# 137 products of constants added to TensorE's queue, in a transformer block with eight experts

## The chip, the cores and the metric

One core of a Trainium2 chip. The metric is the time of one launch on the device, in microseconds (us). TensorE is called PE, VectorE DVE, ScalarE ACT, GpSimd POOL and SyncE SP, as the profile does.

## The reference, cut to what matters

```
def reference(x, tok_weight, q_proj, k_proj, v_proj, o_proj, wg, W1, b1, W2, b2):
    h = take(tok_weight, x)                       # x 32x128 ids, h 32x128x256 f32
    h = h + attention(layernorm(h), ...)          # 16 heads of 16, causal softmax
    h = h + experts(layernorm(h), ...)
    return h
# experts: logits = xf @ wg (8 experts), top-1, a token's rank within its expert,
#   capacity int(4096 / 8 * 1.25) + 1 = 641; tokens past it give 0
#   y = gelu(xe @ W1 + b1) @ W2 + b2             # 256 -> 1024 -> 256
#   out = y[slot] * softmax weight of the token's expert
```

All of it is float32.

## The kernel before, in words

The kernel runs in two blocks: `attention_phase`, then `expert_phase`. Between them all engines join.

**Attention** takes the 32 sequences in 16 groups of two (`NG` = 16, 256 tokens each). The program is written as 22 steps of 8 slots (`step(n, i)`, `for s in range(UNITS)`), and every engine goes through the same steps in its own queue, with semaphores between them. A group passes through the steps as through a pipeline. On PE, for group g: the four transposes of its normalised rows `xn` (`turn4`, slot 7 of step g-1, L522), its projections Q in slot 1, K in slot 2 and V in slot 7 of step g (`project`, `passes`, L559: twelve matmuls of 256 columns each, as three products of a high and a low part), its scores from slot 4 of step g+1 on (L587 adds the mask `maskb` through an identity, L590 multiplies), the shifted scores (L604) and the products with V (L701) some slots later. Then come, in steps g+3 and g+4, the transposes of the values (`turn_values`, L574), their normalised form `on` (L522), the output projection (L559), and in steps g+4 and g+5 the transposes of the second norm `xn2` (L522), the router's logits (L665, eight matmuls of 8 columns) and in step g+6 the ranks (L673 to L677). In the last steps (19 to 21) only these last parts of groups 15 and 14 are left.

Around PE: ScalarE copies each result out of its bank (`xth`, `qp`, `kp`, `va`, `oth`, `x2t`) and takes the exponential. VectorE makes the low parts (`xtl`, `otl`), the rests (`qr`, `kr`), the statistics, the rows' maxima `mx` of each score bank (L781), and the routing up to `oh` and `pos`. GpSimd makes the third parts of q and k, gathers the embedding rows and stores the routed rows to `slots` by indirect DMA (L366). SP writes the parts of q and k to DRAM and reads them back stacked (`qs`, `ks`, L301); the scores need them. It also writes blank rows to `slots` in steps 0 to 5.

At the start, ahead of step 0: PE transposes the token ids (L528), waits for the four attention weights (`d_w`), transposes them (L534, sixteen transposes) and the biases (L538), then the rows of group 0.

**Experts**: eight in turn. For each, `xs` rows are loaded, normalised (`xne`, L1153) and transposed on PE (`turn`, L1071, three turns of four transposes), split into high and low parts (`xh`, `xl`), multiplied with W1 (L1110, sixteen units of six matmuls of 324 columns) and, after the gelu, with W2 (L1127, four of 24), transposed back (L1083), and stored by indirect DMA (L993). The turns of an expert run within the expert before it; those of expert 0 stand alone, ahead of its first matmul. ScalarE and VectorE split the weights (L1008, L1145).

`trib` is a 128x128 bf16 triangle of ones and `maskb` a 128x4x128 bf16 mask. Both are made by GpSimd at the start (`g_set` counts). `bPV` and `bS[0]` are banks of PSUM: the product with V first writes `bPV` in step 3; the scores last write `bS[0]` in step 17.

Of the kernel before, what the change touches and what calls it, by code (L numbers as in the profile page):

```python
# [21 lines left out]
P = 128  # L22
F32 = mybir.dt.float32
F32R = mybir.dt.float32r
BF16 = mybir.dt.bfloat16
# [49 lines left out]
def lm_block(nc, x, table, wq, wk, wv, wo, wg, W1, b1, W2, b2, out):  # L75
    NB, S = x.shape
    D = table.shape[1]
    E, _, F = W1.shape
    H, DK = 16, D // 16
    N = NB * S  # L80
    CAP = int(N / E * 1.25) + 1
    KC = D // P
    GB = 2
    NG = NB // GB
    GT = GB * S
    QUADS = H // 4
    PARTS = 3
    KS_ROWS = 6 * DK
    SCALE = float(DK) ** -0.5
    NT = 6  # L90
    TS = -(-CAP // NT)
    TS += TS % 2
    SL = NT * TS
    NH = SL // 2
    FC = F // P
    NOWHERE = 1 << 20
    assert S == P and TS <= P and NH <= 512

    slots = nc.dram_tensor("rows_of_slots", [E * SL, ROW], F32)
    qparts = [nc.dram_tensor(f"q_parts{i}", [PARTS, D, GT], BF16) for i in range(RING)]  # L100
    kparts = [nc.dram_tensor(f"k_parts{i}", [PARTS, D, GT], BF16) for i in range(RING)]
    outf = out.rearrange("b s d -> (b s) d")

    with ExitStack() as whole:
        def sb_in(scope):
            return lambda name, shape, dt: scope.enter_context(nc.sbuf_tensor(name, shape, dt))

        sb = sb_in(whole)

        def sem(name):  # L110
            return whole.enter_context(nc.semaphore(name))

        bank = {n: whole.enter_context(nc.psum_tensor(n, [P, 512], F32))
                for n in ("S0", "S1", "C0", "C1", "PV", "M0", "M1", "M2")}
        bS = [bank["S0"], bank["S1"]]
        bC = [bank["C0"], bank["C1"]]
        bPV, bM0, bM1, bM2 = bank["PV"], bank["M0"], bank["M1"], bank["M2"]

        identf = sb("identf", [P, P], F32)
        raw = [sb(f"w_raw{q}", [P, 2 * KC * F], F32) for q in range(2)]  # L120

        biases = sb("biases", [P, E * (FC + KC)], F32)
        halfneg = sb("halfneg", [P, 8], F32)
        d_raw = [sem(f"d_raw{q}") for q in range(2)]

        def load_w1(eng, e, q):

            eng.dma_start(raw[q][:, 0:KC * F].rearrange("p (k f) -> p k f", k=KC),
                          W1[bass.ds(e, 1)].rearrange("a (k p) f -> p (a k) f", p=P)).then_inc(d_raw[q], 16)

        def load_w2(eng, e, q):

            eng.dma_start(raw[q][:, KC * F:].rearrange("p (c d) -> p c d", c=FC),
                          W2[bass.ds(e, 1)].rearrange("a (c p) d -> p (a c) d", p=P)).then_inc(d_raw[q], 16)

        load_half = (load_w1, load_w2)

        attention_phase(nc, sb_in, sem, locals())
        expert_phase(nc, sb_in, sem, locals())


def attention_phase(nc, sb_in, sem, v):
# [15 lines left out]
    with ExitStack() as scope:  # L158
        sb = sb_in(scope)

        identb = sb("identb", [P, P], BF16)
        maskb = sb("maskb", [P, 4, S], BF16)
        trib = sb("trib", [P, P], BF16)
        onesb = sb("onesb", [P, P], BF16)
        eps_of = sb("eps_of", [P, GB * E], I32)
        iota8 = sb("iota8", [P, GB, E], F32)
# [349 lines left out]
        def _(pe):  # L516
# [6 lines left out]
                return last  # L523


            pe.wait_ge(g_set, 1)
            pe.wait_ge(v_xf, 1)
            pe.transpose(bM0[:, 0:NB], xf[:, :], identf[0:NB, 0:NB]).then_inc(pe_id, 1)  # L528
            pe.wait_ge(d_w, 64)
            for m in range(4):  # L530
                dst = [bM1, bM2, bS[0], bS[1]][m]
# [9 lines left out]
            pe.wait_ge(v_idt, 1)  # L541
            pe.wait_ge(v_xn, 1)
            turn4(bM0, xn).then_inc(pe_T, 1)

            pe.wait_ge(a_wh, 4)
            pe.wait_ge(v_wl, 4)
# [30 lines left out]
            def step(n, i):  # L577
                for s in range(UNITS):

                    g, u = shift_unit(n, i, s, S_LAG)  # L580
                    if g:
                        if u == 0:
# [50 lines left out]
                    g = group(n, i + 1)  # L633
                    if g and s == 7:
                        wait(pe, v_xn, g.times(1, 1))
                        wait(pe, v_qr, g.times(1))
                        wait(pe, v_on, g.back(4).times(GB, 1))
                        turn4(bM0, xn).then_inc(pe_T, 1)
# [64 lines left out]
                        last.then_inc(pe_PV, 1)  # L703

            steps(pe, step)

        @block.vector
        def _(dve):
# [202 lines left out]
def expert_phase(nc, sb_in, sem, v):  # L911
    D, E, KC, F, FC, SL, NT, TS, NH, N = (v[n] for n in ("D", "E", "KC", "F", "FC", "SL", "NT", "TS", "NH", "N"))
    slots, outf = v["slots"], v["outf"]
    bS, bC, bPV, bM0, bM1, bM2 = (v[n] for n in ("bS", "bC", "bPV", "bM0", "bM1", "bM2"))
    identf, biases, raw, d_raw, load_half = (v[n] for n in ("identf", "biases", "raw", "d_raw", "load_half"))
    up_bank = [bS[0], bS[1], bC[0], bC[1]]
    down_bank = [bPV, bM2]
    turn_bank = [bM0, bM1]
# [8 lines left out]
    with ExitStack() as scope:  # L927
# [133 lines left out]
        @block.tensor  # L1061
        def _(pe):
            def turn(e, r):

                wait(pe, v_exn, e.times(NT, 2 * r + 2))

                wait(pe, v_xl, e.times(TURNS, r // 2))
                for k in range(KC):
                    for j in range(2):
                        at = (k * 2 + j) * TS  # L1070
                        last = pe.transpose(turn_bank[r % 2][:, at:at + TS], xn[:, 2 * r + j, k * P:(k + 1) * P],  # L1071
                                            identf[0:TS, 0:TS])
                last.then_inc(e_turn, 1)

            def back(e, j):


                wait(pe, a_yt, e.times(DOWN, KC * (1 + j // (NT // 2))))
                wait(pe, v_ys, e.times(NT, j - 1))
                if j < 2:  # L1080
                    wait(pe, a_gelu, e.times(NU, NU))
                for c in range(KC):
                    last = pe.transpose(back_bank[j % 2][0:TS, c * P:(c + 1) * P], yt[:, c, j * TS:(j + 1) * TS],  # L1083
                                        identf[:, :])
                last.then_inc(e_back, 1)


            for r in range(TURNS - 1):
                turn(expert(0, 0), r)

            def step(n, i):
                e, e0, e1 = expert(n, i), expert(n, i - 1), expert(n, i + 1)
                q = e.slot
                w1 = [w[q][:, 0:KC * F].rearrange("p (k f) -> p k f", k=KC) for w in (wh, wl)]
                w2 = [w[q][:, KC * F:].rearrange("p (c d) -> p c d", c=FC) for w in (wh, wl)]
                xt = [xh[q], xl[q]]
                ht = [hh, hl]
                three = ((0, 0), (0, 1), (1, 0))
                for u in range(NU):
                    half, f = divmod(u, FC)  # L1100

                    wait(pe, v_xl, e.times(TURNS, TURNS - 1 + half))
                    wait(pe, v_wel, e.times(PIECES, PIECES // 2))
                    wait(pe, a_gelu, e.times(NU, u - 3))
                    if u in (2, 3):

                        wait(pe, v_ys, e.times(NT, u - 3))
                    terms = [(k, a, b) for k in range(KC) for a, b in three]
                    for m, (k, a, b) in enumerate(terms):
                        last = pe.matmul(up_bank[u % 4][:, 0:NH], w1[a][:, k, f * P:(f + 1) * P],  # L1110
                                         xt[b][:, k, half * NH:(half + 1) * NH],
                                         start=(m == 0), stop=(m == len(terms) - 1))
                    last.then_inc(e_up, 1)
                    if isinstance(n, int) and i == 0 and u == 0:
                        turn(e, TURNS - 1)
                    if e0:
                        for j in ((3, 4), (5,))[u] if u < 2 else ():
                            back(e0, j)
                for v in range(DOWN):
                    half, d = divmod(v, KC)  # L1120

                    wait(pe, v_hl, e.times(NU, FC * (half + 1)))
                    wait(pe, v_wel, e.times(PIECES, PIECES))
                    wait(pe, a_yt, e.times(DOWN, v - 1))
                    terms = [(c, a, b) for c in range(FC) for a, b in three]
                    for m, (c, a, b) in enumerate(terms):
                        last = pe.matmul(down_bank[v % 2][:, 0:NH], w2[a][:, c, d * P:(d + 1) * P],  # L1127
                                         ht[b][:, c, half * NH:(half + 1) * NH],
                                         start=(m == 0), stop=(m == len(terms) - 1))
                    last.then_inc(e_down, 1)  # L1130
                    for j in ((), (), (0, 1), (2,))[v]:
                        back(e, j)
                    if e1 and v < TURNS:
                        turn(e1, v)

            steps(pe, step)
            for j in (3, 4, 5):
                back(expert(0, E - 1), j)
# [99 lines left out]
```

## Time and profile before

| what | us |
|---|---|
| median of 3 runs | 629.72 |
| lowest and highest | 628.26, 635.33 |
| the profiled execution's own time | 628.89 |
| its span, first to last instruction | 627.2 |
| PE busy | 557.2 |
| DVE busy | 418.6 |
| ACT busy | 348.1 |

The mean granted clock of PE over the span is 0.947 of 2.4 GHz. A busy PE counts the time in which a matmul was in flight; it can be busy at either of two clock levels, which the page shows in a line of its own. An idle time in brackets behind a row of the timeline is that of the engine just before the row, with what ended it.

### The profile page before, as it was taken

Reading aid. Unit: us, or ns where it says so; the run is one execution under the profiler, and the core shown is the slowest. Engines: PE = TensorE matmul, PEld = TensorE weight load, DVE = VectorE, ACT = ScalarE, POOL = GpSimd, SP = SyncE. Lnnn points to the kernel's source line nnn. Section 1 sums busy time; section 2 is a strip of 40 time slices with the busy share of each in tenths; the row PEclk is TensorE's granted clock in tenths of the full one; section 3 lists DMA queues with packets and bytes.
Section 4 is the critical chain, followed back from the end, with each engine's and each line's share of the span. In section 5 each row is a group of like instructions: output and inputs, shape, how many; then the busy total and the mean of one; then the engine's idle time right before and its main releaser. Section 6 shows DMA issues by size and latency. Waiting matters only on the chain. (4 is left out here: it accounts for less than half of the span.)

```text
span 627.2 us, 14064 instructions
## 1 busy us (share of the span) xinstructions
PE 557.2 (89%) x5179; PEld 497.8 (79%) x5234; DVE 418.6 (67%) x1073; ACT 348.1 (56%) x708; POOL 258.4 (41%) x316
## 2 busy tenths in 40 slices
PE   3678999999999999999976079999999999999993
PEld 3666777777778877777655069999999999999993
DVE  6356679988888988887664256565656565656521
ACT  2225555555655555564441248585858585858550
POOL 5447677765555566655552100404040404040403
PEclk9779999999999999999995569999999999999998
DMA  4698777656667655445111222151515151511101
GB/s 123 168 287 289 252 221 242 203 161 215 193 219 231 185 187 163 148 133 161 52 45 43 78 83 87 31 182 37 180 35 179 33 178 32 179 36 45 33 2 31
DMA packets 42580, 84.37 MB, mean 135 GB/s; under 512 B 6822, under 2 KB 32987, under 8 KB 38864
## 3 DMA queue, kind: packets, MB, share of 16 engines
q1 hardware_dynamic: 35600, 70.66, 35.2%
q0 software_dynamic: 6144, 12.67, 6.4%
q8 instruction: 43, 0.70, 0.5%
q14 instruction: 25, 0.20, 0.1%
q10 hardware_dynamic: 768, 0.13, 0.1%
HBM read 52.64 MB, written 31.74 MB: 135 GB/s over the span
## 5 line engine op out<-in xcount | busy, mean ns | idle before, releaser
L993 POOL DMA_INDIRECT out_dram<-ys,xs x48 | 51.0, 1063 | 221.2 <-DVE ys L1183 211.7
L400 POOL TENSOR_SCALAR_AFFINE_SELECT pt<-pt 128x512 f32<-128x512 f32 x128 | 81.3, 637 | 78.9 <-ACT pt L442 78.0
L442 ACT ACTIVATE pt<-C 128x512 f32<-128x512 f32 x128 | 76.4, 597 | 64.3 <-PE C L604 63.7
L1196 DVE TENSOR_TENSOR hl<-gl,hh 128x324 fp32r<-128x324 f32 x128 | 63.3, 495 | 37.5 <-ACT hh L1033 36.7
L781 DVE TENSOR_REDUCE mx<-S 128x4 f32<-128x512 f32 x128 | 86.5, 680 | 2.7 <-PE S L590 2.4
L590 PE MATMUL S<-ks,qs 96*128 96x128 bf16 x512 | 50.3, 220 | 10.5 <-issue 6.4
L1033 ACT ACTIVATE hh<-gl 128x324 fp32r<-128x324 f32 x128 | 58.6, 464 | 0.0
L701 PE MATMUL PV<-pt,va 128*32 128x128 f32 x1024 | 54.1, 285 | 0.9 <-ACT os L449 0.8
L590 PEld LDWEIGHTS S<-ks,qs 96*128 96x128 bf16 x512 | 40.2, 98 | 15.7 <-issue 0.8
L604 PE MATMUL C<-qs,ks 97*128 97x128 bf16 x512 | 49.8, 219 | 0.0
L1183 DVE SCALAR_TENSOR_TENSOR ys<-C,xs 108x256 f32<-108x256 f32 x48 | 21.8, 481 | 40.1 <-PE C L1083 40.1
L1145 DVE TENSOR_TENSOR wel<-w_raw,weh 128x512 fp32r<-128x512 f32 x64 | 41.0, 684 | 9.4 <-ACT weh L1008 9.4
L559 PE MATMUL M<-xth,wh 128*128 128x256 f32 x128 | 40.4, 316 | 4.1 <-DVE xtl L788 4.1
L1110 PE MATMUL S<-xh,weh 128*128 128x324 f32 x128 | 41.8, 326 | 1.3 <-DVE xl L1159 1.3
L1008 ACT ACTIVATE weh<-w_raw 128x512 fp32r<-128x512 f32 x64 | 36.5, 627 | 10.4 <-PEq L158 10.4
L1127 PE MATMUL M<-hh,weh 128*128 128x324 f32 x128 | 41.0, 321 | 0.0
L1110 PE MATMUL C<-xh,weh 128*128 128x324 f32 x128 | 40.7, 318 | 0.0
L1110 PE MATMUL S<-xl,weh 128*128 128x324 f32 x128 | 40.5, 316 | 0.0
L1110 PE MATMUL S<-xh,wel 128*128 128x324 f32 x128 | 40.4, 315 | 0.0
L1127 PE MATMUL PV<-hh,weh 128*128 128x324 f32 x128 | 40.3, 315 | 0.0
L1110 PE MATMUL C<-xl,weh 128*128 128x324 f32 x128 | 40.2, 314 | 0.0
L1110 PE MATMUL C<-xh,wel 128*128 128x324 f32 x128 | 40.1, 313 | 0.0
(151 smaller groups left out, 1677.3 us busy)
## 6 DMA issues: line engine op xcount, KB each, us to landing
w_raw<-in_L_ffn_W_dram SPq DMA_DIRECT2D x16, 1024.0 KB, 8.6
qs<-q_parts SPq DMA_DIRECT2D x48, 256.0 KB
ks<-k_parts SPq DMA_DIRECT2D x48, 256.0 KB, 5.1
q_parts<-qp SPq DMA_DIRECT2D x16, 384.0 KB, 2.4
k_parts<-kp SPq DMA_DIRECT2D x16, 384.0 KB, 2.5
rows_of_slots<-w_raw SPq DMA_DIRECT2D x6, 877.5 KB, 8.7
xs<-rows_of_slots SPq DMA_DIRECT2D x8, 658.1 KB
out_dram<-h SPq DMA_DIRECT2D x16, 256.0 KB, 5.4
```

Source lines behind the costliest of these rows:

```text
L400: pool.affine_select(out=buf[:, :, :], in_=buf[:, :, :], compare_op=ALU.is_ge, fill=0.0, base=0, pattern=[[0, 4], [1, S]], channel_multipl ...
L442: act.activation(pt[u % 4][:, :, :], bC[u % 2][:, :].rearrange("p (j t) -> p j t", j=4), ACT.Exp, scale=SCALE).then_inc(a_exp, 1)
L590: last = pe.matmul(dst[:, j * S:(j + 1) * S], qs[g.slot][0:KS_ROWS, hh, b * S:(b + 1) * S], ks[g.slot][0:KS_ROWS, hh, b * S:(b + 1) * S], ...
L604: last = pe.matmul(bC[u % 2][:, j * S:(j + 1) * S], ks[g.slot][:, hh, b * S:(b + 1) * S], qs[g.slot][:, hh, b * S:(b + 1) * S], start=True ...
L701: last = pe.matmul(bPV[32 * j:32 * j + 32, (u % QUADS) * S:(u % QUADS + 1) * S], va[g.slot][:, b, hh, :], pt[u % 4][:, j, :], start=True, ...
L781: dve.tensor_reduce(mx[g.slot][:, 4 * (u % QUADS):4 * (u % QUADS) + 4, u // QUADS], bS[u % 2][:, :].rearrange("p (j t) -> p j t", j=4), AX ...
L993: pool.indirect_dma_start(out=outf, out_offset=bass.IndirectOffsetOnAxis(ap=xs[e.slot][:, j, D + 3:D + 4].bitcast(U32), axis=0), in_=ys[j] ...
L1033: act.activation(hh[:, f, cols], gl[u % 4][:, :], ACT.Copy).then_inc(a_hh, 1)
L1110: last = pe.matmul(up_bank[u % 4][:, 0:NH], w1[a][:, k, f * P:(f + 1) * P], xt[b][:, k, half * NH:(half + 1) * NH], start=(m == 0), stop=( ...
L1127: last = pe.matmul(down_bank[v % 2][:, 0:NH], w2[a][:, c, d * P:(d + 1) * P], ht[b][:, c, half * NH:(half + 1) * NH], start=(m == 0), stop ...
L1145: dve.tensor_tensor(wl[q][:, c * PC:(c + 1) * PC], raw[q][:, c * PC:(c + 1) * PC], wh[q][:, c * PC:(c + 1) * PC].bitcast(F32), ALU.subtrac ...
L1196: dve.tensor_tensor(hl[:, f, cols], gl[u % 4][:, :], hh[:, f, cols].bitcast(F32), ALU.subtract).then_inc(v_hl, 1)
```

## The change

PE gets 137 products more: `trib` times `maskb`, 128x128 by 128x512 in bf16, written to a bank that nobody reads. Each starts and stops its own sum, and none waits for or signals a semaphore. They stand:

- 9 ahead of the wait for the attention weights (with a wait for `g_set` at 3, when `trib` and `maskb` are made), and 7 behind the transposes of group 0's rows
- 14 in step 0, slot 7, behind the wait for `xn` of group 1 and ahead of its transposes; 6 in slot 1 and 8 in slot 4 of step 1
- in step 19 (`NG + 3`) 2, 3, 6 and 3 at the head of slots 1, 3, 5 and 6; in step 20 4, 4 and 3 at slots 1, 5 and 6; in step 21 4 at slot 1
- 32 behind the last step of attention
- 22 at the start of the experts' block, and 5 behind each of the first two turns of expert 0

`trib` and `maskb` move from attention's own scope to the outer one, so that they live on in the expert phase. Nothing is removed, and no other engine's program changes.

```diff
--- before.py
+++ after.py
@@ -117,6 +117,7 @@
         bPV, bM0, bM1, bM2 = bank["PV"], bank["M0"], bank["M1"], bank["M2"]
 
         identf = sb("identf", [P, P], F32)
+        trib, maskb = sb("trib", [P, P], BF16), sb("maskb", [P, 4, S], BF16)
         raw = [sb(f"w_raw{q}", [P, 2 * KC * F], F32) for q in range(2)]
 
         biases = sb("biases", [P, E * (FC + KC)], F32)
@@ -159,8 +160,7 @@
         sb = sb_in(scope)
 
         identb = sb("identb", [P, P], BF16)
-        maskb = sb("maskb", [P, 4, S], BF16)
-        trib = sb("trib", [P, P], BF16)
+        trib, maskb = v["trib"], v["maskb"]
         onesb = sb("onesb", [P, P], BF16)
         eps_of = sb("eps_of", [P, GB * E], I32)
         iota8 = sb("iota8", [P, GB, E], F32)
@@ -523,9 +523,19 @@
                 return last
 
 
+            def idle_work(bank, count):
+
+                for _ in range(count):
+                    pe.matmul(bank[:, :], trib[:, :], maskb[:, :, :], start=True, stop=True)
+
+            FILL = {(1, 1): 6, (1, 4): 8, (NG + 3, 1): 2, (NG + 3, 3): 3, (NG + 3, 5): 6, (NG + 3, 6): 3,
+                    (NG + 4, 1): 4, (NG + 4, 5): 4, (NG + 4, 6): 3, (NG + 5, 1): 4}
+
             pe.wait_ge(g_set, 1)
             pe.wait_ge(v_xf, 1)
             pe.transpose(bM0[:, 0:NB], xf[:, :], identf[0:NB, 0:NB]).then_inc(pe_id, 1)
+            pe.wait_ge(g_set, 3)
+            idle_work(bPV, 9)
             pe.wait_ge(d_w, 64)
             for m in range(4):
                 dst = [bM1, bM2, bS[0], bS[1]][m]
@@ -541,6 +551,7 @@
             pe.wait_ge(v_idt, 1)
             pe.wait_ge(v_xn, 1)
             turn4(bM0, xn).then_inc(pe_T, 1)
+            idle_work(bPV, 7)
 
             pe.wait_ge(a_wh, 4)
             pe.wait_ge(v_wl, 4)
@@ -577,6 +588,7 @@
             def step(n, i):
                 for s in range(UNITS):
 
+                    idle_work(bPV if i < NG else bS[0], FILL.get((i, s), 0))
                     g, u = shift_unit(n, i, s, S_LAG)
                     if g:
                         if u == 0:
@@ -633,6 +645,8 @@
                     g = group(n, i + 1)
                     if g and s == 7:
                         wait(pe, v_xn, g.times(1, 1))
+                        if g.off == 1:
+                            idle_work(bPV, 14)
                         wait(pe, v_qr, g.times(1))
                         wait(pe, v_on, g.back(4).times(GB, 1))
                         turn4(bM0, xn).then_inc(pe_T, 1)
@@ -703,6 +717,7 @@
                         last.then_inc(pe_PV, 1)
 
             steps(pe, step)
+            idle_work(bS[0], 32)
 
         @block.vector
         def _(dve):
@@ -912,7 +927,8 @@
     D, E, KC, F, FC, SL, NT, TS, NH, N = (v[n] for n in ("D", "E", "KC", "F", "FC", "SL", "NT", "TS", "NH", "N"))
     slots, outf = v["slots"], v["outf"]
     bS, bC, bPV, bM0, bM1, bM2 = (v[n] for n in ("bS", "bC", "bPV", "bM0", "bM1", "bM2"))
-    identf, biases, raw, d_raw, load_half = (v[n] for n in ("identf", "biases", "raw", "d_raw", "load_half"))
+    identf, biases, raw, d_raw, load_half, trib, maskb = (
+        v[n] for n in ("identf", "biases", "raw", "d_raw", "load_half", "trib", "maskb"))
     up_bank = [bS[0], bS[1], bC[0], bC[1]]
     down_bank = [bPV, bM2]
     turn_bank = [bM0, bM1]
@@ -1085,8 +1101,15 @@
                 last.then_inc(e_back, 1)
 
 
+            def idle_work(count):
+
+                for _ in range(count):
+                    pe.matmul(bPV[:, :], trib[:, :], maskb[:, :, :], start=True, stop=True)
+
+            idle_work(22)
             for r in range(TURNS - 1):
                 turn(expert(0, 0), r)
+                idle_work(5)
 
             def step(n, i):
                 e, e0, e1 = expert(n, i), expert(n, i - 1), expert(n, i + 1)
```

## Rows read from the trace of the kernel before

**Rows 1.** The page: PE's granted clock in 40 slices of 15.7 us.

```profile
PEclk9779999999999999999995569999999999999998
```

**Rows 2.** Busy time by stretch; PEclk 1.00 is 2.4 GHz, 0.50 is 1.2 GHz.

```profile
core 0: us, PE busy (x) PEld busy (x) DVE busy (x) ACT busy (x) POOL busy (x), PEclk, DMA share, GB/s
26.50:31.20 4.70, 4.70 (x23) 4.70 (x23) 0.69 (x1) 1.23 (x2) 1.30 (x3) 0.50 1.04 260
34.90:41.60 6.70, 6.00 (x30) 4.84 (x31) 3.50 (x10) 1.01 (x2) 4.48 (x5) 0.50 0.86 252
325.90:346.60 20.70, 11.67 (x63) 9.64 (x59) 10.87 (x58) 2.92 (x7) 5.70 (x7) 0.56 0.13 45
361.90:372.80 10.90, 7.98 (x31) 7.28 (x32) 5.61 (x13) 4.19 (x8) 0.00 (x0) 0.50 0.03 11
```

**Rows 3.** PE in order of time, 0 to 60 us.

```profile
start us, us, engine line op out<-in xcount [idle before <-releaser]
...
7.36 1.97 PE L534 MATMUL M<-identf,w_raw 128*128 128x128 f32 x8 [4.13 <-DMA w_raw<-in_L_attn_o_proj_dram]
...
11.58 0.63 PE L522 MATMUL M<-identf,xn 128*128 128x128 f32 x4 [0.46 <-DVE xn L752]
14.31 0.51 PE L559 MATMUL M<-xth,wh 128*128 128x256 f32 x1 [2.10 <-DVE xtl L788]
...
16.75 0.41 PE L559 MATMUL M<-xth,wl 128*128 128x256 f32 x1
...
18.76 0.28 PE L559 MATMUL M<-wh,xth 128*128 128x256 f32 x1
...
20.07 0.28 PE L559 MATMUL M<-wh,xtl 128*128 128x256 f32 x1
24.01 0.66 PE L522 MATMUL M<-identf,xn 128*128 128x128 f32 x4 [3.66 <-DVE xn L752]
26.16 0.55 PE L559 MATMUL M<-xth,wh 128*128 128x256 f32 x1 [1.50 <-DVE xtl L788]
...
33.68 0.39 PE L590 MATMUL S<-ks,qs 96*128 96x128 bf16 x4 [2.08 <-DMA ks<-k_parts]
...
42.65 0.35 PE L559 MATMUL M<-xth,wh 128*128 128x256 f32 x1 [0.30 <-DVE xtl L788]
...
46.89 0.38 PE L587 MATMUL S<-maskb,identb 128*128 128x512 bf16 x1 [0.18 <-issue]
```

**Rows 4.** GpSimd in order of time, 0 to 4 us.

```profile
2.68 0.50 POOL L354 TENSOR_SCALAR_AFFINE_SELECT trib<-trib 128x128 bf16<-128x128 bf16 x1
```

**Rows 5.** ScalarE and the SP queue in order of time, 29 to 40 us.

```profile
29.11 0.60 ACT L456 ACTIVATE qp<-M 128x512 bf16<-128x512 f32 x1 [3.81 <-PE M L559]
...
38.55 1.83 SPq L301 DMA_DIRECT2D ks<-k_parts  x3
```

**Rows 6.** The tile ks, 20 to 75 us: its DMAs.

```profile
DMA to landing us min/median/max: 4.6/5.3/6.3
```

**Rows 7.** PE in order of time, 320 to 346.6 us.

```profile
323.62 1.06 PE L665 MATMUL M<-wgs,x2t 128*128 128x8 f32 x8
...
328.03 0.18 PE L673 MATMUL M<-oh,trib 128*128 128x8 bf16 x1 [2.07 <-DVE oh L877]
...
330.16 1.12 PE L522 MATMUL M<-identf,on 128*128 128x128 f32 x4 [0.81 <-DVE on L804]
332.78 0.55 PE L559 MATMUL M<-wh,oth 128*128 128x256 f32 x1 [1.50 <-DVE otl L788]
...
337.21 1.87 PE L665 MATMUL M<-wgs,x2t 128*128 128x8 f32 x8 [0.69 <-ACT x2t L465]
...
341.50 1.09 PE L522 MATMUL M<-identf,xn 128*128 128x128 f32 x4 [1.02 <-DVE xn L752]
```

**Rows 8.** Line 158, where attention's block ends: the engines' sequencers.

```profile
L158 PEldq DRAIN  x1: 335/335/335, 346.3 to 346.3; - x1
...
L158 POOLq DRAIN  x1: 7165/7165/7165, 348.9 to 348.9; - x1
```

**Rows 9.** PE in order of time, 346.6 to 367 us.

```profile
361.97 0.98 PE L1071 MATMUL M<-identf,xne 108*128 108x108 f32 x4 [15.43 <-DVE xne L1153]
364.54 0.98 PE L1071 MATMUL M<-identf,xne 108*128 108x108 f32 x4 [1.58 <-DVE xne L1153]
```

## The prediction

> **What bounds the kernel now.** I read the page first for the shape: TensorE (PE) is busy 557.2 of 627.2 us (the table above), 89%, and the line of granted clock shows where its slow stretches lie [rows 1]: 7 to 9 tenths in the first three slices, 5 and 6 tenths in slices 21 to 24, full elsewhere. Between 64 and 320 us, and from 373 us on, PE is fed and fast, and nothing that the change touches lies there. So the stake is three places: the head (to about 60 us), the tail of attention (328 to 346.6 us) and the start of the experts (362 to 373 us). The stretches [rows 2] give the level in each: 0.50, that is 1.2 GHz and not 2.4, with PE busy all of 26.5 to 31.2, 6.00 of 6.70 us in 34.9 to 41.6, 11.67 of 20.7 in the tail and 7.98 of 10.9 at expert 0. Then I read PE's instructions in order of time [rows 3, 7]. In the tail each one waits for a result made from the one before it, so PE's durations lie on the path. In the head the score matmuls of step 1 wait for a DMA (2.08 us, to 33.68) [rows 3], so there PE's speed is only partly on the path.
>
> **The price of one idle product.** It has 512 columns. Twelve projection matmuls of 256 columns start between 14.31 and 16.75 at the low clock, and the last twelve of this stage between 18.76 and 20.07 at the high one [rows 3]: one each 2.44/11 = 0.22 us and 1.31/11 = 0.119 us. A product of 512 bf16 columns is taken at twice that: 0.44 low, 0.24 high. 137 are added. The weight load of each hides behind the one before. They write a bank nobody reads then, so no other engine waits for them; what is queued behind them is PE's own next work.
>
> **What the high clock gives back.** Four transposes take 0.66 us high (at 24.01) and 1.12 low (at 330.16); eight router matmuls 1.06 (323.62) and 1.87 (337.21) [rows 3, 7]; projections 0.119 and 0.22. That is 41, 43 and 46% less; I take 43%.
>
> **Ahead of the weights (9) and after the first transposes (7).** The 9 start when GpSimd's constants are ready, at 2.68 + 0.50 = 3.2 us [rows 4], and even low end at 3.2 + 9 x 0.44 = 7.2, before the weights land at 7.36 [rows 3]. They cost nothing. They speed the weight transposes, but the first projection at 14.31 waits for VectorE's xtl, which is at the end of VectorE's own serial work on statistics, rows and weights; so no gain yet. The 7 fill the gap of 2.10 us ahead of 14.31: 1.7 us high, 3.1 low. Before, the clock had fallen by then and Q, K and V of group 0 ran at 0.22 up to 17.6. Held high, Q is 11 x 0.10 = 1.1 us earlier, and with it ScalarE, VectorE, GpSimd and the DMAs behind it: 1.1 to 1.3 us.
>
> **Fourteen in step 0.** They stand behind the wait for xn and ahead of the transposes, so they are not in PE's gap of 3.66 us but after it [rows 3]. A gap of 2.10 us had let the clock fall before, so I expect a fall here too, and the 14 to run low for most: 14 x 0.44 = 6.2, against 3.4 if high. The transposes move from 24.01 to 22.8 + 5.6 = about 28.4 (26.2 if high). Behind them: 0.6, then the gap of 1.50 us, in which the 6 of step 1 fit (1.4), then 24 matmuls of Q and K at 0.119 = 2.9, then 8 more products, 1.9. The first scores then start at 28.4 + 0.6 + 1.5 + 2.9 + 1.9 = 35.3 (33.1 if high), against 33.68, which was a wait for a DMA. From 33.68 to the next Q at 42.65 [rows 3] the clock was low with PE 90% busy; held high, V's 12 matmuls, four transposes and the mask matmuls save about 2.0. So Q of group 2 starts at 42.3 or 40.1. The cover is thin, though: group 1's Q reaches ScalarE at 29.11 before, and after at about 28.4 + 2.1 + 1.4 + 0.2 = 32.1, 3 us late, its K some 2.2 late; the stacks of its keys are issued from 38.55 on, three in 1.83 us, and land 5.3 us (4.6 to 6.3) after their issue [rows 5, 6]: before at about 45.1, after at 47.3, where the scores of group 1 started at 46.89. So a new wait of about 0.5 to 1 us comes where 0.4 to 2 were gained. **Head: 0, between -2.5 (gain) and +2.5.**
>
> **The last two groups (2+3+6+3, 4+4+3, 4).** The gaps are 2.07, 0.81, 1.50, 0.69 and 1.02 us [rows 7], that of 0.69 met twice, and the two later waits for VectorE's oh are alike; the products take 0.5, 0.7, 1.4, 0.7 and 0.95 high: all fit. Low they take 0.9, 1.3, 2.6, 1.3 and 1.8: all but the first overrun, by 0.5 to 1.1 each, 4.7 us together. Held high, the tail's 11.67 us of busy PE [rows 2], less 1.0 for the rank matmuls and the rim, shrinks by 43%: **4.6 us**, all on the path, since ScalarE's copy, VectorE's routing and GpSimd's two stores all start from it. The open point is whether the clock holds over the first gap, of which only 0.5 of 2.07 us is filled: before, it fell right there. I take it that it mostly holds, as PE's idle time is 1.6 instead of 2.07 and all later gaps close.
>
> **Thirty-two at the end of attention.** What the engines join on is GpSimd's drain, which ends at 348.9 + 7.2 = 356.1; PE's own drain is over at 346.6 [rows 8]. So 9.5 us cover them: 7.7 high, 14.1 low. High they cost nothing; wholly low 4.6.
>
> **Expert 0 (22, then 5 and 5).** The rows land late, so the first transpose is at 361.97 [rows 9]. The 22 start at the join, 356.1, and take 5.3 (to 361.4) or 9.7 (to 365.8). The fives take 1.2 (or 2.2) each; the first gap is 1.58 [rows 9], and I take the second for alike. Held high, the 7.98 us of busy PE [rows 2] lose 44%: 3.5 us, on the path, as PE starts expert 0 and never waits again. But between the end of the 32 and the join PE is idle for about 2 us (moved up with the tail: 341.9 + 7.7 = 349.6 to 351.5), which is as long as the gaps that let the clock fall before. Then 8 to 16 of the 22 run low (the low stretches of the head lasted 3.4 to 6.8 us): 1.6 to 3.2 more, less 0.6 of slack. **Expert start: gain 3.5 - 1.4 = 2.1, between 0.9 and 3.5.**
>
> **A rule against it.** Between 7.36 and 11.58 us PE did transposes only, and they went from 0.25 us apiece (eight in 1.97) to 0.13 to 0.16 (four in 0.63) [rows 3], so here transposes did bring the clock up. The Trainium skill ("TensorE: Matmul & The Clock Gate", Part 4: PE-mode transpose) says that full rate does not engage for transpose-mode, which counts as less than busy. By that rule the tail, with its many transposes, would stay low around the few products; the trace speaks against it.
>
> **The sum.** The profiled execution took 628.89 (span 627.2 and 1.7 around it); 628.89 - 0 - 4.6 - 2.1 = 622.2. It lies 0.8 below the median of the three runs, 629.72, so I say **623.0**. A measurement of this kernel can tell about 1% from no change: 6.3 us, so "faster" starts at 623.4.
>
> **The rivals.**
> - *The clock falls once in the tail* at the first gap and is back a stretch later, since low products overrun the gaps and leave PE no idle time. Of the tail's 4.6 us, 2.3 are left: 625.3. For it: the same gap let it fall before, and 1.6 us of it stay. Chance 0.22; same.
> - *The head costs*: the 14 products push group 1's Q and K behind the DMA queue, which was near full there (share 0.86 to 1.04 in [rows 2]), by 2.5 us and the steps after it inherit that: 625.5, or 627.5 with the former. Chance 0.14; same.
> - *All holds*: the clock survives both the step-0 gap and the join. Head -2, expert 3.5: 628.89 - 10.1 = 618.8, as a median 619.6. Chance 0.12; faster.
> - *Slower: the products do not hold the clock.* If constants in bf16 are no work to it, every product costs 0.44: steps 0 and 1 8 us (6.2 for the 14, 1.1 beyond the gap for the 6, 3.5 for the 8, less the 2.08 of waiting), tail 4.7, join 4.6, expert start 3.8 + 0.6 + 1, the 7 another 1: 628.9 + 23.7 = 652.6, as a median 653. It decides in the tail: from the point where over half of it runs low with the products in it, the tail costs more than it gives. Against: transposes and matmuls alike were followed by a rise in the head. Chance 0.02.
> - *The tail alone stays low*, since it is mostly transposes: 4.7 of overrun and 4.6 at the join, expert's 2.1 gained: 628.9 + 7.2 = 636.1, as a median 637. Chance 0.03. This is what the rule of the Trainium skill named above would do here.
>
> The forecast itself has 0.47, of which I put 0.30 under 623.4. Faster 0.30 + 0.12 = 0.42; slower 0.05, and 0.02 for the head and the tail going wrong together by more than I priced; the rest, 0.51, within 1%. The range takes in all but the last two and the ends of the head's cost: 618 to 630.
>
> **What would show it.** Granted clock 1.00 from 329 to 346 and 0.4 to 0.5 us shorter transposes at the last groups; the join 4 to 5 us earlier; GpSimd's drain still its last arrival; a fall in the gap before expert 0's products and the first expert matmul with 324 columns at high clock from the start; the transposes of group 1 at 26 to 28.4 and the scores of group 1 waiting for keys. Wrong if the clock is 0.50 in the tail, if PE's drain comes after GpSimd's, or if Q of group 2 comes later than 42.65.

## The result, and the profile after

Over 20 runs of each, taken in turn, the change takes 627.76 us (623.69 to 630.41) and before 632.58 (628.26 to 635.33). The ratio is 0.9927, interval 0.9909 to 0.9946: 4.6 us less (the two medians lie 4.8 apart). The median of before's first three runs, on which the prediction stands, was 629.72, 2.9 lower than that of the twenty; so the forecast of 623.0 was one of 0.989, 6.7 us less. The profiled execution after took 626.09 us, its span is 624.4 and the mean granted clock 0.987.

The page's line of granted clock after answers to [rows 1]. The three low slices, 21 to 23 counted from 0, are gone; of the first ones some is left:

```profile
PEclk9897999999999999999999999999999999999997
```

Busy time by stretch after: the two low stretches of the head, then the tail and the start of expert 0, which answer to the last two of [rows 2]:

```profile
24.00:27.60 3.60, 3.60 (x11) 1.38 (x10) 0.00 (x0) 0.00 (x0) 2.50 (x3) 0.55 1.04 299
51.60:57.90 6.30, 5.81 (x33) 5.42 (x35) 2.07 (x4) 2.38 (x4) 3.52 (x5) 0.50 0.86 232
330.90:347.10 16.20, 13.07 (x87) 7.73 (x88) 10.94 (x56) 2.92 (x7) 5.50 (x7) 1.00 0.14 51
362.50:373.40 10.90, 10.11 (x63) 8.34 (x65) 6.99 (x14) 6.29 (x13) 0.00 (x0) 1.00 0.10 19
```

The tail is at 1.00 throughout and 16.2 us long, where it was 20.7 at 0.56; PE is busier (13.07 us) by the products. Expert 0 is at 1.00 with PE busy 10.11 of 10.9. In the head a low stretch remains at 24 to 27.6, and another stands at 51.6 to 57.9, in steps 2 and 3, where this execution of before was high.

PE in order of time after, 0 to 60 us, beside [rows 3]. L529 are the products, L570 the projections, L599 the mask, L616 the shifted scores:

```profile
3.29 3.82 PE L529 MATMUL PV<-maskb,trib 128*128 128x512 bf16 x9
7.36 1.09 PE L544 MATMUL M<-identf,w_raw 128*128 128x128 f32 x8 [0.24 <-issue]
...
12.11 1.67 PE L529 MATMUL PV<-maskb,trib 128*128 128x512 bf16 x7
14.38 0.36 PE L570 MATMUL M<-xth,wh 128*128 128x256 f32 x1 [0.60 <-DVE xtl L803]
...
23.06 4.66 PE L529 MATMUL PV<-maskb,trib 128*128 128x512 bf16 x13 [4.16 <-DVE xn L767]
27.55 0.60 PE L522 MATMUL M<-identf,xn 128*128 128x128 f32 x4
...
29.65 0.36 PE L570 MATMUL M<-xth,wh 128*128 128x256 f32 x1 [0.21 <-DVE xtl L803]
...
34.34 0.38 PE L599 MATMUL S<-maskb,identb 128*128 128x512 bf16 x1
...
41.54 0.36 PE L570 MATMUL M<-xth,wh 128*128 128x256 f32 x1 [0.67 <-issue]
...
46.87 0.38 PE L599 MATMUL S<-maskb,identb 128*128 128x512 bf16 x1 [1.26 <-DMA ks<-k_parts]
...
51.87 0.61 PE L616 MATMUL C<-qs,ks 97*128 97x128 bf16 x4 [1.01 <-DMA qs<-nm]
```

The 9 take 0.42 us each, the low price, although the granted clock is given as 1.00 there (3.3 to 7.1 us): for these first microseconds the durations and that line disagree. They end before the weights land; the sixteen transposes behind them take half as long (eight in 1.09, before 1.97), and the first projection starts at 14.38, before 14.31. The 14 run from 23.06 to 27.55, mostly low, behind a gap of 4.16 us. The transposes of group 1 then start at 27.55 instead of 24.01, the first scores at 34.34 instead of 33.68, Q of group 2 at 41.54 instead of 42.65. The scores of group 1 start at 46.87, before 46.89, and now wait 1.26 us for the DMA of its keys. The keys are hardly later for it: their stacks were issued from 38.55 on in before and are issued 0.4 us later here, so it is PE that comes sooner.

```profile
38.96 1.82 SPq L301 DMA_DIRECT2D ks<-k_parts  x3
```

One more wait, for the shift row of qs, is 1.01 us long, and behind it the clock is low.

The tail, the join and expert 0 after, PE in order of time, beside [rows 7] and [rows 9] (L687 ranks, L529 and L1107 products, L1087 turns, L1133 first expert matmul):

```profile
332.90 0.18 PE L687 MATMUL M<-oh,trib 128*128 128x8 bf16 x1 [1.53 <-DVE oh L892]
...
334.98 0.66 PE L522 MATMUL M<-identf,on 128*128 128x128 f32 x4 [0.53 <-DVE on L819]
...
346.88 0.18 PE L687 MATMUL M<-oh,trib 128*128 128x8 bf16 x1 [0.25 <-DVE oh L892]
...
347.02 7.07 PE L529 MATMUL S<-maskb,trib 128*128 128x512 bf16 x31
356.99 4.91 PE L1107 MATMUL PV<-maskb,trib 128*128 128x512 bf16 x22 [2.91 <-PEq L159]
362.54 0.59 PE L1087 MATMUL M<-identf,xne 108*128 108x108 f32 x4 [0.64 <-DVE xne L1176]
...
366.57 0.42 PE L1133 MATMUL S<-xh,weh 128*128 128x324 f32 x1 [0.18 <-DVE xl L1182]
...
381.40 0.30 PE L1150 MATMUL PV<-hh,weh 128*128 128x324 f32 x1
```

The same places in before that no row above shows, the last rank matmul, the first matmul with W1 (L1110) and the first with W2 (L1127; L1150 after):

```profile
346.25 0.19 PE L673 MATMUL M<-oh,trib 128*128 128x8 bf16 x1 [1.10 <-DVE oh L877]
...
366.78 0.64 PE L1110 MATMUL S<-xh,weh 128*128 128x324 f32 x1 [1.26 <-DVE xl L1159]
...
384.20 0.30 PE L1127 MATMUL PV<-hh,weh 128*128 128x324 f32 x1
```

And the drains at the join, beside [rows 8]:

```profile
L159 POOLq DRAIN  x1: 7168/7168/7168, 349.5 to 349.5; - x1
L159 PEldq DRAIN  x1: 4050/4050/4050, 350.1 to 350.1; - x1
```

From the first rank matmul to the last it is 332.90 to 346.88, 13.98 us, where before it was 328.03 to 346.25, 18.2 us. PE's drain waits out the 32 and ends at 350.1 + 4.05 = 354.2, GpSimd's at 349.5 + 7.2 = 356.7: it is still the last. The 22 stand in a gap that would have been 5.6 us, behind 2.91 us of idle time in which the clock did not fall. The first expert matmul starts 9.9 us after the join's drain, before 366.78 - 356.1 = 10.7.

This pair of traces alone would mislead. With the change the tail's first rank matmul comes 4.9 us later (332.90, before 328.03), so the join, which was to come 4 to 5 us earlier, comes at 356.7 against 356.1. VectorE's residual sum of group 0 (L846; with the change L861) marks the end of the head. VectorE in order of time, before and then after:

```profile
81.10 0.69 DVE L846 TENSOR_TENSOR h<-M,h 128x512 f32<-128x512 f32 x1
```

```profile
84.74 0.69 DVE L861 TENSOR_TENSOR h<-M,h 128x512 f32<-128x512 f32 x1
```

3.6 us of it are there by 85 us. The other 1.3 come at 129 us, far from any product, in one wait of PE for VectorE's xtl:

```profile
129.42 0.36 PE L570 MATMUL M<-xth,wh 128*128 128x256 f32 x1 [1.26 <-DVE xtl L803]
```

A like delay of 0.7 to 1.3 us stands there in three of the twelve traces, two of them of the full change; its cause stays open. How much of the 3.6 is the change is what the first experiments ask.

### The profile page after: what moved, and what is told of

It is laid out like the page before. It is cut to its first block and busy times, and to the rows that moved or that the text cites. A ratio compares the mean times of both kernels' runs of the same rounds, so it can differ in the third digit from the quotient of the medians.

```text
span 624.4 us, 14332 instructions
## 1 busy us (share of the span) xinstructions
PE 576.3 (92%) x5311; PEld 498.5 (80%) x5371; DVE 419.6 (67%) x1073; ACT 338.8 (54%) x708; POOL 258.3 (41%) x316
## 5 line engine op out<-in xcount | busy, mean ns | idle before, releaser
L1049 ACT ACTIVATE hh<-gl 128x324 fp32r<-128x324 f32 x128 | 61.7, 491 | 0.0
L602 PEld LDWEIGHTS S<-ks,qs 96*128 96x128 bf16 x512 | 40.1, 98 | 15.7 <-issue 0.6
L616 PE MATMUL C<-qs,ks 97*128 97x128 bf16 x512 | 50.3, 220 | 1.0 <-DMA qs<-nm 1.0
L1055 ACT ACTIVATE gl<-S,biases 128x324 f32<-128x324 f32 x64 | 34.7, 544 | 16.0 <-PE S L1133 11.8
L1024 ACT ACTIVATE weh<-w_raw 128x512 fp32r<-128x512 f32 x64 | 36.9, 645 | 10.5 <-PEq L159 10.5
L1133 PE MATMUL S<-xh,weh 128*128 128x324 f32 x128 | 41.1, 321 | 0.2 <-DVE xl L1182 0.2
L570 PE MATMUL M<-xth,wh 128*128 128x256 f32 x128 | 38.6, 301 | 2.7 <-DVE xtl L803 2.1
L1150 PE MATMUL M<-hh,weh 128*128 128x324 f32 x128 | 41.0, 321 | 0.0
L1150 PE MATMUL PV<-hh,weh 128*128 128x324 f32 x128 | 40.3, 315 | 0.0
L1133 PE MATMUL C<-xh,weh 128*128 128x324 f32 x128 | 40.2, 314 | 0.0
L1150 PE MATMUL M<-hl,weh 128*128 128x324 f32 x128 | 40.0, 312 | 0.0
L1150 PE MATMUL PV<-hl,weh 128*128 128x324 f32 x128 | 40.0, 312 | 0.0
L1133 PE MATMUL C<-xl,weh 128*128 128x324 f32 x128 | 40.0, 312 | 0.0
```

Source lines behind the costliest of these rows:

```text
L602: last = pe.matmul(dst[:, j * S:(j + 1) * S], qs[g.slot][0:KS_ROWS, hh, b * S:(b + 1) * S], ks[g.slot][0:KS_ROWS, hh, b * S:(b + 1) * S], ...
L616: last = pe.matmul(bC[u % 2][:, j * S:(j + 1) * S], ks[g.slot][:, hh, b * S:(b + 1) * S], qs[g.slot][:, hh, b * S:(b + 1) * S], start=True ...
L1049: act.activation(hh[:, f, cols], gl[u % 4][:, :], ACT.Copy).then_inc(a_hh, 1)
```

## The experiments

All ratios are to before, run on the same chip in turn; 1% is 6.3 us. The first four versions ran on one chip, the next four on a second, the last two on a third, so differences between versions of different sets carry the noise of both ratios. Each diff is shortened and is against the kernel after, unless it says otherwise. The line behind each diff is what was on record ahead of the run.

**Without the head's products, and the head's alone.**

```diff
-            idle_work(bPV, 9)
-            idle_work(bPV, 7)
-            FILL: (1, 1): 6, (1, 4): 8
-                        if g.off == 1:
-                            idle_work(bPV, 14)
```

> Without the 44 products of the head (9, 7, 14, 6, 8); tail, join and expert 0 keep theirs. Theory A (the head costs and the rest gives): the profiled pair lost 3.6 us in the head and won 4.2 in the tail and 3.4 at expert 0, so this runs 7 to 8 us under before, ratio 0.988. Theory B (head neutral, the rest gives 4.6 in all): ratio 0.993, as the full change.

Measured: 0.9904 (0.9879 to 0.9930), 6.0 us less than before. That lies between the two theories, and the interval holds both.

```diff
-            FILL: all of NG + 3, NG + 4, NG + 5
-            idle_work(bS[0], 32)
-            idle_work(22)
-                idle_work(5)
```

> Only the 44 products of the head. Theory A: 3 us over before, ratio 1.005. Theory B: within 1 us of it, ratio 0.999 to 1.001.

Measured: 1.0006 (0.9986 to 1.0026). Theory A, drawn from one pair, falls as a size: the head alone costs 0.4 us (-0.9 to 1.6) and not 3. The version without the head's products has the same head as before, and its residual sum of group 0 starts at 83.19 us, 2.1 later than in before's own trace:

```profile
83.19 0.69 DVE L857 TENSOR_TENSOR h<-M,h 128x512 f32<-128x512 f32 x1
```

So before's profiled execution had a fast head. The execution decides this: in that of before the clock was high from 42 to 62 us; in that of the version without the head's products it was low from about 49 to 56 us, with the same program there but for one wait.

The same version shows the open point of the tail. PE in order of time (L683 ranks, L522 transposes):

```profile
330.11 0.18 PE L683 MATMUL M<-oh,trib 128*128 128x8 bf16 x1 [1.53 <-DVE oh L888]
...
332.19 1.11 PE L522 MATMUL M<-identf,on 128*128 128x128 f32 x4 [0.52 <-DVE on L815]
...
345.31 0.18 PE L683 MATMUL M<-oh,trib 128*128 128x8 bf16 x1 [0.25 <-DVE oh L888]
```

The transposes of `on` took 1.11 us, the low price: the clock had fallen again, 2.1 us behind the first rank matmul (granted clock 0.50 from 332.2 on); it was back at 335.7, and the tail from first to last rank matmul is 15.20 us instead of 13.98. Such a fall came in four of the seven traces with 2 products in the gap ahead of the first rank matmul (15.20, 14.97, 15.13 and 15.20 us; 13.98 to 13.99 in the other three).

**The 14: taken out, moved, doubled.**

```diff
                         wait(pe, v_xn, g.times(1, 1))
-                        if g.off == 1:
-                            idle_work(bPV, 14)
```

> The full change without the 14 ahead of the transposes of group 1. Theory A1 (the delay of those transposes, and so of group 1's keys, is what costs): as the version without the head or better, ratio 0.986 to 0.989. Theory A2 (the 8 ahead of the first scores, or the 6, cost too): ratio 0.990 to 0.992.

Measured: 0.9920 (0.9895 to 0.9944). A1 is outside the interval. A2 holds the value at its upper end, but so does no effect at all: beside the full change (0.9927 and 0.9923) nothing can be told.

```diff
+                        if g.off == 1:
+                            idle_work(bPV, 14)
                         wait(pe, v_xn, g.times(1, 1))
-                        if g.off == 1:
-                            idle_work(bPV, 14)
```

> The full change with the 14 moved ahead of the wait for xn, into the gap of 3.7 to 4.2 us, where at the high clock they take 3.1. If the place of the 14 is the fault: no delay of the transposes, and the clock holds from 12 us on: ratio 0.985 to 0.988, better than without them. If the clock's hold in the head is worth nothing since DMAs set its pace: as without them, 0.988.

Measured: 0.9902 (0.9874 to 0.9930), above both expectations, though the interval reaches down to the second, and about 1.5 us under the full change, which the intervals don't separate. Its trace says why a faster head brings so little. ScalarE, PE and the SP queue in order of time, 28 to 40 us:

```profile
28.31 0.58 ACT L456 ACTIVATE kp<-M 128x512 bf16<-128x512 f32 x1
...
31.53 0.36 SPq L312 DMA_DIRECT2D k_parts<-kp  x1
...
32.11 0.59 PE L599 MATMUL S<-maskb,identb 128*128 128x512 bf16 x1 [2.55 <-DMA ks<-k_parts]
...
35.44 1.82 SPq L301 DMA_DIRECT2D qs<-q_parts  x3
...
37.30 1.86 SPq L301 DMA_DIRECT2D ks<-k_parts  x3
```

Group 1's K is ready for ScalarE at 28.31, before at 31.63. Its third part is written from 31.53 on, 3.3 us earlier than before (34.87). But the queue issues the stacks only when the writes have landed: qs at 35.44, ks at 37.30, 1.25 us earlier than the 38.55 of [rows 5]. The wait of the SP queue for the landing of q's parts, 28 to 45 us, first in this version and then in before:

```profile
SPq L301 <- DMA q_parts<-qp: 3.5, 1, 3.5
```

```profile
SPq L301 <- DMA q_parts<-qp: 1.4, 1, 1.4
```

The write was issued at 29.66, 2.7 us earlier than before's (32.35), and took 5.8 us to the next issue, where before's took 4.3. So most of what PE won went into this wait. The first scores wait for a DMA till 32.11, and those of group 1 start at 45.50, 1.4 us earlier than the 46.89 of [rows 3].

```diff
-                            idle_work(bPV, 14)
+                            idle_work(bPV, 28)
```

> The full change with 28 products where the 14 stand. If they delay the keys of group 1 and this delay is on the path: 3 us more than the full change, about 2 us under before, ratio 0.997. If the delay hides behind the DMAs: as the full change, 0.993.

Measured: 0.9974 (0.9954 to 0.9994), 3.0 us slower than the full change. PE in order of time:

```profile
22.72 8.75 PE L529 MATMUL PV<-maskb,trib 128*128 128x512 bf16 x28 [3.98 <-DVE xn L767]
...
33.41 0.36 PE L570 MATMUL M<-xth,wh 128*128 128x256 f32 x1 [0.21 <-DVE xtl L803]
...
45.30 0.36 PE L570 MATMUL M<-xth,wh 128*128 128x256 f32 x1 [0.67 <-DVE xtl L803]
...
50.28 0.38 PE L599 MATMUL S<-maskb,identb 128*128 128x512 bf16 x1 [0.91 <-issue]
```

The 28 took 8.75 us, the first 5.1 of them at the low clock (granted 0.50 from 22.7 to 27.8). From one trace to the other the second 14 move the first projection of group 1 from 29.65 to 33.41, Q of group 2 from 41.54 to 45.30 and the scores of group 1 from 46.87 to 50.28. The measured 3.0 us are what 14 cost at 0.22, as if the second 14 lay wholly on the path, but the value is known to about 1.7 us either way, and in the traces the residual sum of group 0 comes at 86.18 us, 1.4 and 1.9 later than in the two of the full change (84.74, 84.28). That the first 14 had used up the cover is argued from this, not shown.

**Tail and expert 0 each alone.**

```diff
-            idle_work(bPV, 9), (bPV, 7), (bPV, 14), FILL (1, 1), (1, 4)
-            idle_work(22)
-                idle_work(5)
```

> Before with the 29 products of the last three steps and the 32 at the end alone. The version without the head's products gained 6.0 us. If tail and expert 0 each give what the profiles show (3 to 4.2 and 2.6 to 3.4): 3.3 us under before, ratio 0.995, and expert 0 runs low or high by whether the clock outlives the 3 us of idle time ahead of the join. If the tail's gain is an artefact of one pair: 0.998 or more.

Measured: 0.9946 (0.9921 to 0.9970), 3.4 us. Without the 22 PE is idle from 348.4 till 357.4, and the clock falls in it. Busy time by stretch, then PE in order of time:

```profile
350.00:352.00 2.00, 0.00 (x0) 0.00 (x0) 0.06 (x1) 0.72 (x2) 0.00 (x0) 1.00 0.00 0
353.00:363.00 10.00, 2.75 (x11) 2.08 (x12) 4.87 (x12) 3.62 (x7) 0.00 (x0) 0.50 0.37 124
```

```profile
357.41 0.98 PE L1083 MATMUL M<-identf,xne 108*128 108x108 f32 x4 [9.02 <-DVE xne L1170]
```

```diff
-            idle_work(bPV, 9), (bPV, 7), (bPV, 14), FILL (1, 1), (1, 4)
-            FILL: all of NG + 3, NG + 4, NG + 5
```

> Before with the 32 at the end, the 22 and the 5 and 5 alone. By the same sum: 2.7 us under before, ratio 0.9957. The forecast's term was 2.1, with a fall of the clock at the join; if the clock does not fall there, 3.4.

Measured: 0.9971 (0.9947 to 0.9994), 1.8 us. The parts add up: 3.4 + 1.8 - 0.4 = 4.8 against 4.6 for the whole, each of them known to 1.2 to 1.6 us. The 32 stand in both versions.

**The gaps filled further, and step 2.**

```diff
 the version with the 14 ahead, and
-            FILL: (NG + 3, 1): 2
+            FILL: (NG + 3, 1): 7
-            idle_work(bS[0], 32)
+            idle_work(bS[0], 41)
```

> The version with the 14 moved ahead, and two gaps filled further: 7 for 2 in the first gap of the tail (2.07 us), 41 for 32 at the end. If the clock sometimes falls in the tail because that gap is open: 1 us under the version with the 14 ahead, ratio 0.988. If PE's drain then comes after GpSimd's: the same or worse, 0.990 or more.

Measured: 0.9908 (0.9874 to 0.9942), no different from the version that it is built on (0.9902, on another chip). In its trace the tail held the clock and took 13.99 us; in the one of the 14 ahead it held too, so one fall of 1.2 us in some executions is all that there was to win there, and the timing can't show it. At the join PE was idle for 0.96 us, not 2.91, and the clock held; so it did in the version that follows. PE in order of time in its head:

```profile
38.92 0.36 PE L570 MATMUL M<-xth,wh 128*128 128x256 f32 x1 [0.67 <-DVE xtl L803]
...
45.62 0.38 PE L599 MATMUL S<-maskb,identb 128*128 128x512 bf16 x1 [2.63 <-issue]
...
46.17 0.63 PE L599 MATMUL S<-maskb,identb 128*128 128x512 bf16 x1
```

Here the head was high from the weight transposes up to 46 us: Q of group 2 starts at 38.92, 3.7 us earlier than before. Then PE waits 2.63 us ahead of the scores of group 1, which start at 45.62, 1.3 us earlier than before. 2.4 of the 3.7 us were given back in one wait, and right behind it the clock fell: the mask product at 45.62 still takes 0.38 us, that at 46.17 takes 0.63, the low price.

```diff
 the version with the gaps filled, and
+            FILL: (2, 4): 10, (2, 7): 4
```

> The version with the gaps filled, and two more places: 10 products in step 2, slot 4, ahead of the wait for the keys of group 1 (a gap of 2.6 us in its trace, in which the clock fell at 46 us), and 4 in slot 7. If that fall costs what low matmuls between 46 and 56 us show, 2 us less than the version with the gaps filled, ratio 0.986. If the DMAs set the pace of step 2 and 3 anyway: the same, 0.990.

Measured: 0.9887 (0.9861 to 0.9914). PE in order of time:

```profile
46.33 2.32 PE L529 MATMUL PV<-maskb,trib 128*128 128x512 bf16 x10
...
52.94 0.40 PE L616 MATMUL C<-qs,ks 97*128 97x128 bf16 x4 [0.70 <-DMA qs<-nm]
```

The clock stayed high from 40 us on, but the chain of DMAs came later in this execution (the scores of group 1 start at 48.49, behind the 10 products), and the residual sum of group 0 was at 82.59 against 82.67. Whether the two tenths of a per cent between 0.9908 and 0.9887 are real stays open: it is 1.3 us, and the two intervals allow anything from 4 us less to 1.4 more.

> The full change once more, for a second look at its trace and to stand beside the version above on the same chip: ratio 0.991 to 0.995. If the loss of 3.6 us in the head of the first pair of traces was between executions and not the change, this trace reaches the residual sum of group 0 nearer to 82 than to 84.7 us.

The full change once more, no edit. Measured: 0.9923 (0.9900 to 0.9946). PE in order of time:

```profile
46.59 0.38 PE L599 MATMUL S<-maskb,identb 128*128 128x512 bf16 x1 [1.26 <-DMA ks<-k_parts]
...
51.58 0.61 PE L616 MATMUL C<-qs,ks 97*128 97x128 bf16 x4 [1.25 <-DMA qs<-nm]
```

The wait for the keys of group 1 (1.26 us, to 46.59) and that for the shift row (1.25 us) are there again, and the residual sum of group 0 is at 84.28 us, against my expectation of 82. So part of the 3.6 us was the change after all: the three traces with the 14 where they stand show 84.74, 84.28 and 84.19 us; without them, or with them ahead, 82.11 to 82.67; before's head in four executions 81.10, 83.19, 80.25 and 83.27. That is a mean of 84.4 against 82.0 for before's head, 2.4 us, while the timed runs of the head alone say 0.4 (up to 1.6). What the clock did in steps 2 and 3 goes with half of it. The two executions of before's head that stayed high there are the early ones (81.10 and 80.25); the two in which the clock fell, from 49 or 50 to 56 or 57 us, are the late ones (83.19 and 83.27). The three with the 14 all had a fall between 51 and 58 us. Against before's head with the fall they are 1.2 us late, which the timed runs allow. Whether the head's products make this fall more frequent, four and three executions can't say.

## Why the prediction was right or wrong

The direction was right, and the time fell in the range, which says little: 618 to 630 is 12 us wide and holds the median of before that it started from. The size was 4.6 us, 0.73%, where 6.7 was said. The chances put 0.51 on "within 1%", which the ratio is in; but the text called 1% what a measurement can tell, and twenty runs told 0.7% from nothing with an interval of 0.2% to each side.

**The level.** 2.9 of the 4.8 us between 623.0 and 627.76 are the base: three runs of before had a median 2.9 under that of twenty. The gain itself came out 2.1 us short (4.6 for 6.7); by the timed parts 1.2 of that is the tail, 0.3 expert 0 and 0.4 the head.

**The price of a product and of the clock** held: 32 in 7.07 us and 22 in 4.91 are 0.22 each (0.24 said), and four transposes of `on` 0.66 for 1.12.

**The tail** is the step that was mis-sized: 4.6 us said, 3.4 measured for tail and join alone (1.9 to 5.0, so by timing alone 4.6 is not excluded; the traces decide it). The working was nearly right for an execution in which the clock holds, 18.2 - 14.0 = 4.2 us; but "I take it that it mostly holds" over the first gap failed in four traces of seven, at 1.0 to 1.2 us each. The tail took 18.2, 18.3 and 17.35 us in the three traces without its products and 14.6 on average in the seven: 3.3 us, as timed. Shown is the fall and its price; that the 1.6 us of open gap bring it about is only argued. With 7 products there the clock held in both traces, but where it holds in three of seven, two in a row come by chance about once in five. That was the first rival, which had 0.22; its loss was put at 2.3, twice what it is, since the clock was back after 3.4 us in each. Also, before's own tail was not always wholly low (17.35 us in the trace of the head alone, with 3.4 us high in it). The rule of the Trainium skill on transposes ("TensorE: Matmul & The Clock Gate", Part 4) found no support: the tail's transposes went by at the high clock, 0.66 us for four. Products stood between them here, so the head of before, where transposes alone went ahead of the rise, says more against it.

**The 32** cost nothing, as said: PE's drain ends 2.5 us ahead of GpSimd's in the trace after. In the trace with expert 0's products alone they ran low for 5.2 us and took 9.63; PE's drain and GpSimd's then ended within 0.1 us of each other, at 358.3, so the cover was just used up.

**Expert 0**: 2.1 said, 1.8 measured (0.4 to 3.3), and 2.6 as the difference between the versions without the head and with the tail alone (6.0 and 3.4). The way was as said: the clock fell at the join in five of the six traces with 32 and 22 products and those of the tail, and the 22 took 6.3 to 6.6 us instead of 4.91; the sixth is that of the result above. PE in order of time in the version without the head's products:

```profile
355.42 6.59 PE L1103 MATMUL PV<-maskb,trib 128*128 128x512 bf16 x22 [2.90 <-PEq L159]
```

From the end of GpSimd's drain to the first W1 matmul it then took 10.5 to 11.0 us, hardly less than without the products (10.7 to 11.4 in three traces), and from there to the first W2 matmul 14.8 instead of 16.5 to 17.4. From the drain to the first W2 matmul that is 27.6 to 28.1 us without the products and 24.7 to 25.9 in the six traces: 2.5 us for the 3.5 - 1.4 of the forecast. The trace of expert 0's products alone shows 27.5 and so almost none of it: PE waited 2.70 us for its rows behind the 22, and the clock fell once more, 367.4 to 370.8. Its execution took 630.5 us, 3.2 over the median of that version.

**The head** was put at 0, between -2.5 and 2.5, and its timed runs say +0.4. The steps were near: transposes at 28.4 said and 27.55 found, first scores 35.3 and 34.34, Q of group 2 42.3 and 41.54, and the new wait for the keys of group 1 is there, 1.26 us. But its working was wrong in one step: the stacks of the keys were to be issued 2.2 us later and were 0.4 later, since the writes ahead of them landed sooner after their issue (q's parts 2.4 us to the next issue, before 4.3). That the 14 run low for most of their time was right. Missed was the fall between 46 and 59 us, in steps 2 and 3: before's profiled execution did not have it, nine of the other eleven traces have one.

**The slower rivals** did not come: with the products of bf16 constants the granted clock in the tail was 1.00, where it was 0.56, and at expert 0 1.00, where it was 0.50.

Two sums of the rivals are slightly off: head and first rival together give 623.0 + 2.3 + 2.5 = 627.8 and not 627.5, and the items of steps 0 and 1 in the slower rival add to 8.7 us and not 8. Neither bears on the forecast. The low slices that it calls 21 to 24 are three, 21 to 23.

## What to carry to other kernels

Idle products are worth their place where PE's own duration is on the path and the gap is longer than they are: here, in the last two groups of attention and ahead of the experts, where they gave 3.4 and 1.8 us. Where a DMA sets the pace the clock buys little: of 3.7 us won in the head 2.4 went into the next wait. Products behind a wait delay what the wait was for (14 more of them cost 3.0 us); ahead of it they are covered, though that the first 14 gain by the move (1.5 us) is not separated from nothing. And don't read a term of 3 us off one pair of traces of a kernel whose executions lie 7 us apart.

## What the runs showed of the hardware

- Executions of one program differ in where the clock falls. Before's head reached the same instruction at 80.25, 81.10, 83.19 and 83.27 us in four traces. In the tail the clock fell in four of seven traces of programs that are the same there.
- The same idle time of 2.90 to 2.91 us at the join was followed by a fall in five traces and not in a sixth (after, ahead of 356.99), and behind one of 2.07 us the clock was down too (before, ahead of 328.03). The length of one gap does not decide it.
- At the join GpSimd's drain takes 7.16 to 7.17 us in every trace, whenever it begins; all engines wait for it, and PE's work behind its last rank matmuls is covered up to about 9.5 us (with 9.63 us of products both drains ended at 358.3).
- A write of q's parts took 2.4, 4.3 and 5.8 us from its issue to the issue that waits for it, the longer the earlier it was issued (34.61, 32.35 and 29.66 us), at a DMA share from 28 to 36 us of 0.66 in after, 0.99 in before and 0.90 in the version with the 14 ahead. Here an earlier issue bought little.
